# Four 32-column groups of TensorE for the squared head norms and the gate products

## The reference, cut to what matters

```python
def softmax_kernel(data, proj, is_query, eps=0.0001):
    data_dash = jnp.einsum('bhnd,md->bhnm', data * normalizer, proj)
    diag = jnp.sum(data ** 2, axis=-1, keepdims=True) * 0.5 * normalizer ** 2
    ...
    return ratio * (jnp.exp(data_dash - diag - m) + eps)
...
scores = jax.nn.softmax(xt @ wg + bg, axis=-1)      # xt 1024x512, wg 512x8
routing_weights, selected_experts = _sparsemixer_eval(scores, E)
```

## Time and profile before

| | |
|---|---|
| median of three runs | 1832.22 us |
| lowest, highest | 1824.89, 1834.66 us |
| the profiled execution | 1830.28 us |
| its span, first to last instruction | 1828.2 us |
| TensorE busy, granted clock over the span | 93%, 0.974 |
| DVE, POOL, ACT busy | 60%, 55%, 37% |
| records of line 744 (head rows) | 64, 30.0 us busy |
| records of line 754 (head columns) | 32, 2.6 us busy |
| ACT's copy of a bank's 8 rows (line 1272), mean | 587 ns |

### The profile page before, as it was taken

The page is one execution under the profiler, slowest core; times in us unless marked ns, Lnnn a source line. Parts: engine busy times, 40 slices in busy tenths (PEclk is TensorE's granted clock), DMA queues, the critical chain, the costliest instruction groups (busy, mean ns, idle before and its releaser), DMA issues.

```text
span 1828.2 us, 19904 instructions
## 1 busy us (share of the span) xinstructions
PE 1694.3 (93%) x7751; PEld 1303.5 (71%) x7751; DVE 1105.7 (60%) x1846; ACT 675.6 (37%) x880; POOL 1001.3 (55%) x539
## 2 busy tenths in 40 slices
PE   5999999999899999999996899999999589999986
PEld 5765567788765656788885787778787477887863
DVE  7597878999878787744357423433423375533385
ACT  3323544232323443432312565555555222211112
POOL 3336801466788788678732677676767361333312
PEclk9999999999999999999998999999999889999988
DMA  9353201455332222232243877787785511221001
GB/s 340 102 173 75 24 1 50 127 116 116 64 61 21 24 24 1 60 80 47 70 155 120 295 258 250 248 269 253 249 275 188 175 28 47 70 70 48 22 1 46
DMA packets 146507, 212.03 MB, mean 116 GB/s; under 512 B 43724, under 2 KB 60336, under 8 KB 145168
## 3 DMA queue, kind: packets, MB, share of 16 engines
q1 hardware_dynamic: 98464, 176.96, 29.2%
q0 software_dynamic: 42832, 18.84, 8.2%
q10 hardware_dynamic: 5120, 14.99, 2.4%
HBM read 186.69 MB, written 30.08 MB: 119 GB/s over the span
## 4 chain that ended last, share of the span: by engine, by line
PE 78%; DVE 14%; ACT 3%; issue 3%; POOL 1%; DMA 1%; SPq 0%; DVEq 0%; POOLq 0%
PE PS L642 20%; PE PS L644 20%; PE PS L643 20%; PE PS L790 5%; PE PS L817 3%; PE PS L831 3%; PE PS L808 2%; PE PS L744 1%; PE PS L685 1%; POOL slots_x L2385 1%; DVE op_b L1611 1%; DVE h_op L1994 1%; ACT W L1421 1%; DVE kmax L1731 1%; DVE picked L1634 1%
## 5 line engine op out<-in xcount | busy, mean ns | idle before, releaser
L2272 POOL TENSOR_TENSOR W<-raw,W 128x2048 fp32r<-128x2048 f32 x40 | 193.3, 4835 | 291.5 <-ACT W L1187 291.4
L2347 POOL DMA_INDIRECT table_w<-edge_add,edge_ix x128 | 210.5, 1645 | 129.7 <-DMA table_w<-edge_add,edge_ix 76.5
L2347 POOL DMA_INDIRECT table_c<-edge_add,edge_ix x128 | 205.4, 1605 | 55.7 <-issue 34.1
L642 PE MATMUL PS<-op_b,W 128*128 128x512 f32 x576 | 226.4, 393 | 7.2 <-DVE op_b L1611 4.6
L644 PE MATMUL PS<-op_b,W 128*128 128x512 f32 x576 | 224.8, 390 | 0.0
L643 PE MATMUL PS<-op_b,W 128*128 128x512 f32 x576 | 224.8, 390 | 0.0
L642 PE MATMUL PS<-W,op_a 128*128 128x512 f32 x480 | 188.1, 392 | 3.3 <-DVE op_a L1799 1.8
L643 PE MATMUL PS<-W,op_a 128*128 128x512 f32 x480 | 187.1, 390 | 0.0
L644 PE MATMUL PS<-W,op_a 128*128 128x512 f32 x480 | 187.0, 390 | 0.0
L2390 POOL TENSOR_TENSOR W<-raw,W 128x2048 fp32r<-128x2048 f32 x30 | 143.5, 4792 | 44.3 <-ACT W L1421 44.3
L1187 ACT ACTIVATE W<-raw 128x2048 fp32r<-128x2048 f32 x40 | 76.5, 1920 | 160.6 <-PE PS L644 103.4
(11 more groups left out here) (432 smaller groups left out, 3783.0 us busy)
## 6 DMA issues: line engine op xcount, KB each, us to landing
raw<-in_L_ffn_w_dram SPq DMA_DIRECT2D x46, 1024.0 KB, 5.7
raw_e<-in_L_ffn_w_dram SPq DMA_DIRECT2D x22, 1024.0 KB, 5.6
raw_v<-in_L_ffn_w_dram SPq DMA_DIRECT2D x22, 1024.0 KB, 5.1
raw<-in_L_mix_W_dram SPq DMA_DIRECT2D x16, 1024.0 KB, 5.5
raw<-table_c SPq DMA_DIRECT2D x10, 1024.0 KB, 5.1
key_row<-key_dram SPq DMA_DIRECT2D x32, 256.0 KB, 3.9
w_row<-in_edge_weight_dram SPq DMA_DIRECT2D x32, 256.0 KB, 5.1
table_w<-zero POOLq DMA_DIRECT2D x4, 1024.0 KB, 7.9
```

The source lines that it names most:

```text
L642: pe.matmul(ps, lhs_hi, rhs_hi, start=start, stop=False)
L2272: pool.tensor_tensor(lo_at, raw[:, r % 2, :], hi_at.bitcast(F32), ALU.subtract).then_inc(lo_done, 1)
L2347: pool.indirect_dma_start(out=tb, out_offset=bass.IndirectOffsetOnAxis(ap=edge_ix[:, i, c:c + 1].bitcast(U32), axis=0), in_=edge_add[:, i, ...
```

## The change

The four products of `head_rows` no longer add up in the same 8 rows. The stationary matrix is now 128x32 with two columns that are not zero, the same for all four blocks. Block m writes to the 32 partitions from 32m of the bank, that is, to its own group of 32 columns of the array. ACT copies all 128 partitions. `head_columns` picks the 2 of 32 rows of each block while it turns them: a float32 product of `d_rows` (now the stationary operand, 128x128) with the 8 wanted columns of the identity.

The gate does the same with its four blocks of features. The weights stay float32 and unsplit, padded with zeros to 32 columns. Each is multiplied by the high and by the low half of the features as float32 numbers: 8 float32 products in a job, 2 on each group of columns. The turning product sums the four groups through `gate_sel`, a 128x8 matrix of ones and zeros that DVE makes from the identity.

```diff
-        head_sel = place("head_sel", [P, NK, HEADS])
-        d_rows = place("d_rows", [HEADS, N], F32, at_e)
+        head_sel = place("head_sel", [P, COLS])
+        d_rows = place("d_rows", [P, N], F32, at_e)
...
                     for m in range(NK):
-                        mm = pe.matmul(bank(n)[0:HEADS, :], head_sel[:, m, :], G[:, 4 * c + m, :], start=(m == 0), stop=(m == NK - 1))
+                        mm = pe.matmul(bank(n)[m * COLS:(m + 1) * COLS, :], head_sel[:, :], G[:, 4 * c + m, :], start=True, stop=True)
...
-                    mm = pe.transpose(bank(n)[:, t * HEADS:(t + 1) * HEADS], d_rows[:, t * P:(t + 1) * P], ident[0:HEADS, 0:HEADS])
+                    mm = pe.matmul(bank(n)[:, t * HEADS:(t + 1) * HEADS].rearrange("p (m j) -> p m j", j=2), d_rows[:, t * P:(t + 1) * P],
+                                   ident[:, :].rearrange("p (m s) -> p m s", s=COLS)[:, :, 0:2], start=True, stop=True)
...
-                for k in range(NK):
-                    x = slice(k * N + c * HALF, k * N + (c + 1) * HALF)
-                    mm = split_mm(bank(n)[0:EXPERTS, :], wg[:, 0, k, :], wg[:, 1, k, :], op_a[:, 0, x], op_a[:, 1, x],
-                                  k == 0, k == NK - 1)
+                for i in range(2):
+                    for k in range(NK):
+                        x = slice(k * N + c * HALF, k * N + (c + 1) * HALF)
+                        mm = pe.matmul(bank(n)[k * COLS:(k + 1) * COLS, :], wg[:, k, :], op_a[:, i, x].bitcast(F32), start=(i == 0), stop=(i == 1))
...
-                mm = pe.transpose(bank(n)[:, t * EXPERTS:(t + 1) * EXPERTS], gate_T[:, t * P:(t + 1) * P], ident[0:EXPERTS, 0:EXPERTS])
+                mm = pe.matmul(bank(n)[:, t * EXPERTS:(t + 1) * EXPERTS], gate_T[:, t * P:(t + 1) * P], gate_sel[:, :], start=True, stop=True)
...
-                    act.activation(d_rows[:, c * HALF:(c + 1) * HALF], bank(n)[0:HEADS, :], ACT.Copy).then_inc(job_act, 1)
+                    act.activation(d_rows[:, c * HALF:(c + 1) * HALF], bank(n), ACT.Copy).then_inc(job_act, 1)
...
-                act.activation(gate_T[:, c * HALF:(c + 1) * HALF], bank(n)[0:EXPERTS, :], ACT.Copy).then_inc(job_act, 1)
+                act.activation(gate_T[:, c * HALF:(c + 1) * HALF], bank(n), ACT.Copy).then_inc(job_act, 1)
...
-            link(dve.tensor_copy(wg[:, 0, :, :], wg_raw[:, :, :]))
-            dve.tensor_tensor(wg[:, 1, :, :], wg_raw[:, :, :], wg[:, 0, :, :].bitcast(F32), ALU.subtract).then_inc(wg_ready, 1)
+            dve.tensor_reduce(gate_sel[:, :], ident[:, :].rearrange("p (k s) -> p s k", s=COLS)[:, 0:EXPERTS, :], AX_X, ALU.add).then_inc(wg_ready, 1)
...
-            link(pool.memset(head_sel[:, :, :], 0.0))
-            for m in range(NK):
-                pool.memset(head_sel[0:DH, m, 2 * m:2 * m + 1], 0.5 * NORMALIZER ** 2)
-                ins = pool.memset(head_sel[DH:P, m, 2 * m + 1:2 * m + 2], 0.5 * NORMALIZER ** 2)
+            pool.memset(wg[:, :, :], 0.0)
+            link(pool.memset(head_sel[:, :], 0.0))
+            for h in range(2):
+                ins = pool.memset(head_sel[h * DH:(h + 1) * DH, h:h + 1], 0.5 * NORMALIZER ** 2)
...
-            pool.dma_start(wg_raw[:, :, :], a["L0_ffn_wg"].rearrange("(k p) e -> p k e", p=P)).then_inc(gate_loaded, 16)
+            pool.dma_start(wg[:, :, 0:EXPERTS], a["L0_ffn_wg"].rearrange("(k p) e -> p k e", p=P)).then_inc(gate_loaded, 16)
```

More of the change, by code:

```diff
@@ L67 @@
 BANKS = 8
+COLS = 32
 def visit_tiles(v):
@@ L341, in gps_network @@
         ctx_sb = place("ctx_sb", [P, 2, 4, DH])
-        wg_raw = place("wg_raw", [P, NK, EXPERTS])
-        wg = place("wg", [P, 2, NK, EXPERTS], F32R)
+        wg = place("wg", [P, NK, COLS])
+        gate_sel = place("gate_sel", [P, EXPERTS])
         bg = place("bg", [P, EXPERTS])
@@ L383, in gps_network @@
         mean_row = place("mean_row", [P, D], F32, at_v)
-        gate_T = place("gate_T", [EXPERTS, N], F32, at_b)
+        gate_T = place("gate_T", [P, N], F32, at_b)
         deg_sum = place("deg_sum", [P, 4, 256], F32, at_w + slot_of["adj1"] % SLOTS * 8 * BLK)
```

## The result

The changed kernel runs in 1824.74 us (median of 20 runs, 1813.00 to 1829.14), the kernel before in 1829.13 us (20 runs beside it, 1824.16 to 1834.66). The ratio is 0.9972, with a 95% interval of 0.9961 to 0.9982: 5.1 us less (4.4 between the two medians), a real gain, but within the 0.5% that the prediction counts as no change. The forecast was 12.5 us off an execution of 1830.28 us. The profiled execution after took 1821.88 us, 2.9 under its median, while the one before was 1.1 over its own; so the two traces differ by 8.4 us, and 3 to 4 us of that are the choice of executions.

What follows compares the result with a forecast made beforehand. TensorE was taken to bound the kernel (93% busy, 78% of the chain). Gains of 5 + 4.3 + 5.3 = 14.6 us, 12.5 let through, gate 0, gave 1817.8 from the profile, 1819.7 from the median; forecast 1819, range 1809 to 1828.

Steps and rivals of the forecast that it cites:

- Head rows: Norm products on four column groups: 1.0 us a job, so a pair of jobs takes 2.0 instead of 6.96 us.
- head columns: Turning the norms by eight float32 products: 1.8 us, 1.2 us more at each of four places.
- ACT's copies: Copying 128 partitions instead of 8 costs nothing: 598 ns against 587.
- First layer: Norms of q and k and waits at v in the first layer: 5 us gained, bounds 3 to 6.2.
- Second layer: Same places in the second layer, with POOL's subtraction still stopping DVE: 4.3 us gained, bounds 2 and 6.5.
- Gate: Gate products on four groups plus dearer turning: 0 us, between +1.3 and -0.3.
- Given back or found later: Behind the second layer's heads: up to 5.3 us freed at 746.14, with 12.5 of 14.6 us let through in all.
- the escape: DVE passes line 1611 before POOL's subtraction at 746.14, freeing up to 5.3 us; without it 9.3 us remain.
- the cap: At the fifth job of `down`, waits for DVE and ACT's weight load let only 12.5 of 14.6 us through.
- the mixed case: Two more of POOL's subtractions on DVE's path, 4.5 us each, would leave 3.5 us of the gain.
- rival 1: DVE keeps most of the gain at k and v in both layers: only 6 us less, 1826; chance 0.20.

Runs made afterwards that it cites:

- e3_pool: Changed kernel with two pairs of POOL's scatters in layer 1 moved behind up1.0's subtraction: 1813.81 us, ratio 0.9919; run again on another chip 1820.66 us, 0.9945.
- f2_down8: e3_pool with POOL's third batch of scatters cut from 12 to 8, to bring down1.0's subtraction four pairs earlier: 1828.07 us, ratio 0.9997.
- f4_both: The edits of f2_down8 and f3_fill together: 1830.34 us, ratio 1.0012.
- f1_down11: e3_pool with POOL's third batch of scatters cut from 12 to 11, to bring down1.0's subtraction one pair earlier: 1813.90 us, ratio 0.9931.
- f3_fill: Changed kernel plus overwritten products in two TensorE waits, at the first gate job and before layer 0's second job of k's rows: 1823.16 us, ratio 0.9966.
- e4_pool_before: The kernel before, with two pairs of POOL's scatters in layer 1 moved behind up1.0's subtraction: 1825.03 us, ratio 0.9975.

## Why the prediction was right and wrong

**Head rows, head columns, ACT's copies: right.** 1.85 to 1.97 us against 2.0, 1.68 against 1.8, 597 ns against 598. The Trainium skill, "TensorE: Matmul & The Clock Gate", in its section on packing small matmuls, has three column groups of 32 at 2.38 times and weight loads that overlap only where row groups differ. The estimate from it was 1.10 us a job; this trace has 0.93 to 0.98 for four full-height groups, so here the measurement decides against it.

**First layer: right in size.** 4.3 us at the first heads, 6.0 at line 831/833, against 5 (3 to 6.2). DVE's idle before its second square of k fell from 6.34 only to 3.85 us, not 1.3, and TensorE's wait for the last square rose to 4.98 us, as said (some 5). Why the idle did not fall further is open. The 1.7 us of clock behind the first heads were not in the sum. By the other two traces with the norms of before the gain at the first heads is 2.1 to 3.2 us, around the lower bound.

**Second layer: right.** 10.5 - 6.0 = 4.5 us against 4.3 (with 4.3 at the first heads in place of 6.0 it would be 6.2, within the bounds of 2 and 6.5). The stop fell into an edge batch, as worked out (line 1646, 4.85 us).

**Gate: within its bounds in the two traces compared.** 0.7 us slower by the stretch to line 899, between +1.3 and -0.3; over the eight traces it is from 0.4 faster to 1.7 slower. The cause, the low clock on the transposes behind a longer wait, was not foreseen.

**"Given back or found later": the step that failed.** It let 12.5 us through, of which 5.3 (capped to 3.2) came from DVE passing POOL's subtraction at 746. It took DVE's lead of 4.3 us at 746 as given. But in between there is another of POOL's subtractions, at 648.02, which before only brushed line 1724. The prediction worked out the lead relative to POOL at one place and not at the other on the way. The lead was also smaller than its 4.3: 2.4 us (10.3 for DVE, 7.9 for POOL), and that turned a touch into an almost full stop, cost 3.9 us, and with them the escape. By the prediction's own numbers, 9.3 us for DVE and 5 for POOL, DVE would have come to line 1724 0.7 us ahead of POOL, nearly past it.

So its premise that TensorE does not move POOL's queue in the second layer fails too: between the subtractions of wv and wo POOL took 64.0 us in all three traces with the norms of before, and 58.1 to 60.9 in the eight with the new norms and the same queue there. POOL's waits in that stretch are for the transfers of its own scatters; why they are shorter is open.

The kernel with POOL's queue moved shows that the first stop is the cause of the second: take away the first stop, and both are gone, the cap binds at the load of the next weights, and the trace is 9.9 us ahead at the gate. The prediction had named its own disproof, new waits of 4 us and more for DVE between 580 and 760 us; the row at 646.63 with 4.98 us is one.

What came is the mixed case that it mentions in passing behind the rivals: the gains of the layers, less stops. In size the 5.1 us are those of rival 1 (6 us), which had 0.20; but rival 1 let only 6 us reach the heads of the second layer, and 8 to 10.5 did. By the prediction's own limit of 0.5% the result is "same", which had 0.25 against 0.69 for faster. That the time lies inside the stated range is due to the range's width, up to 1828.

**The cap: right in kind, wrong in size and place.** With both stops gone TensorE waits 5.8 us at 763, not at the fifth job of `down`. Taking that wait away did not help (ratio 0.9931, between the 0.9919 and 0.9945 of e3_pool). That POOL's list as a whole is next is what the waits of 10.5 and 8.7 us of f2_down8 and f4_both show; in f1_down11 itself it is 1.12 us.

**The rest.** Of the 12.5 us the traces have 8.4 and the medians 5.1 by ratio. The 3 to 4 us between are the executions that were profiled. Of the eight traces with packed norms and POOL's old order up to wv, two (f1_down11, f3_fill) show TensorE held for 10 us there, and have their first heads of layer 1 at 569.4 instead of 565.8; they are the two of the eight that had passed the stop of line 1814. The kernel before had 7.0 us to spare. How often that happens in executions without a trace is open. The starting median of three runs, 1832.22, was 3 us above that of 20 runs, which is why a forecast that was 7 us too bold in gain is 5.7 us off in time.

## What to carry to other kernels

An engine whose queue runs mostly at its own pace (here POOL's scatters and subtractions) is a row of obstacles that hardly move with the others. When the others move ahead by a few us, each obstacle on the way has to be checked again, the ones that hardly touched the path before above all; one stop also takes away the lead that the next was to be passed with. And before moving work ahead, look how many us of slack the slow queue's results have: 7.0 us of it went down to 1.1 here. Last, take more than one trace of the kernel before: three with the same code up to the heads of layer 1 differ by 2.4 us there.

## What the runs showed of the hardware

- Four products of 128x32 stationary and 512 moving columns on four column groups take 0.93 to 0.98 us, little more than one (0.87), and the 8 turning products (16 records) 1.68 us.
- POOL's subtraction of 128x2048 (5.1 to 5.2 us) holds DVE's operations on SBUF to about its own end: by 3.9, 4.5 and 4.7 us at lines 1726, 1613 and 1646 of the changed kernel. The last is a tiny one: 128x8 with one input took 4.85 us instead of 0.17. Beside the subtraction of f2_down8 at 724.16 the four parts of line 1599 (one tensor input, SBUF to SBUF) took 4.32 instead of 2.2 us. Operations that read PSUM went on, as the eight at 589.73 beside POOL's subtraction of 588.85 (0.61 us each, lines below). The Trainium skill, "GPSIMD Engine Reference", section on specifications, names this contention for DVE instructions with two SBUF inputs or in a 2-port mode; the traces agree for those with two inputs (lines 1726 and 1613). Whether the ones with one input ran in such a mode no trace shows.
- The same wait does not always bring the same clock: behind 2.63 us of idle at the gate the 16 transposes took 1.97 us in two traces, 2.64 to 2.73 in two and 3.49 to 3.63 in four. Behind 0.92 and 1.7 us they took 1.97 in all five. In layer 0 of the kernel before the second job of the norms of k took 5.30 us behind a wait of 2.44, partly at the low clock, and in e4_pool_before 3.60 behind the same wait. What decides between these cases is open.
- The 16 transposes of h_tok some 70 us later took 3.68, 3.38 and 3.41 us in the three traces with the gate of before, behind waits of 3.33, 3.31 and 2.18 us, and 1.97 in seven of the eight with the packed gate and no filling products, behind waits of 2.65 to 3.32 us. That gave the changed kernel's trace 1.7 us that were in no sum; why is open.
- POOL took 64.0 us from the subtraction of wv to that of wo in three traces and 58.1 to 60.9 in eight, with the same 13 pairs of scatters between them; a single scatter's transfer took up to 9.5 us (f4_both, at 525.84).

The lines of the changed kernel that the second point speaks of, POOL and DVE (start us, us, engine, line):

```profile
588.85 5.14 POOL L2273 TENSOR_TENSOR W<-raw,W 128x2048 fp32r<-128x2048 f32 x1
589.73 4.87 DVE L1760 TENSOR_SCALAR E_T<-PS 128x512 f32<-128x512 f32 x8
```
